# Second attention: four value products side by side for the first column half too, the odd key blocks' part collected on its own and added once per four head pairs

## What is computed

```python
def split_heads(y):
    return y.reshape(B, T, H, hd).transpose(0, 2, 1, 3)
q = split_heads(x @ Wq)          # H = 16 heads of hd = 16
k = split_heads(x @ Wk)
v = split_heads(x @ Wv)
scores = jnp.einsum('bhqd,bhkd->bhqk', q, k) / jnp.sqrt(jnp.float32(hd))
scores = jnp.where(causal, scores, jnp.float32(-jnp.inf))
attn = jax.nn.softmax(scores, axis=-1)
out = jnp.einsum('bhqk,bhkd->bhqd', attn, v)
```

## Time and profile before

| | |
|---|---|
| median of three runs | 853.15 us (852.07 to 854.26) |
| the profiled execution | 851.88 us, of which 850.1 us are its span |
| TensorE matmul | 759.7 us busy, 89% of the span |
| VectorE | 530.4 us, 62% |
| ScalarE | 430.0 us, 51% |
| GpSimd | 423.9 us, 50% |
| second attention, first exponential to last copy | about 487.6 to 619 us of the span |
| experts' block | from about 619.3 us |

### The profile page before, as it was taken

The page is one execution under the profiler, slowest core; times in us unless marked ns, Lnnn a source line. Parts: engine busy times, 40 slices in busy tenths (PEclk is TensorE's granted clock), DMA queues, the critical chain, the costliest instruction groups (busy, mean ns, idle before and its releaser), DMA issues. The chain is left out here.

```text
span 850.1 us, 12826 instructions
## 1 busy us (share of the span) xinstructions
PE 759.7 (89%) x3664; PEld 366.5 (43%) x3664; DVE 530.4 (62%) x1350; ACT 430.0 (51%) x922; POOL 423.9 (50%) x746
## 2 busy tenths in 40 slices
PE   2948999999999999984984798999889999999995
PEld 2332223222222222221752232333267888888883
DVE  3659777777777876603661876788147555555555
ACT  1431566665666665661133065767744554455552
POOL 1751556664334223422132032235368998689994
PEclk9975899999999999995888598999999999999997
DMA  6393740010011001012029374233232221122221
GB/s 186 128 295 87 156 103 18 25 55 20 15 47 40 14 22 58 17 46 71 1 94 272 119 181 122 72 110 117 79 84 80 66 69 60 39 68 67 62 63 58
DMA packets 60074, 69.82 MB, mean 82 GB/s; under 512 B 14904, under 2 KB 40857, under 8 KB 60010
## 3 DMA queue, kind: packets, MB, share of 16 engines
q1 hardware_dynamic: 59936, 69.08, 29.1%
q10 hardware_dynamic: 80, 0.07, 0.0%
HBM read 47.35 MB, written 15.47 MB: 74 GB/s over the span
## 5 line engine op out<-in xcount | busy, mean ns | idle before, releaser
L715 ACT ACTIVATE top<-ps 128x512 f32<-128x512 f32 (+3 forms) x384 | 171.0, 490 | 134.7 <-PE ps L662 134.5
L662 PE MATMUL ps<-mid 99*128 99x512 bf16 (+3 forms) x576 | 185.5, 338 | 8.4 <-ACT mid L715 5.4
L645 PE MATMUL ps<-mid 96*128 96x512 bf16 (+3 forms) x512 | 174.8, 364 | 13.8 <-PEq L233 9.6
L757 DVE CUSTOM_DVE_ANT_0 ps<-ps,keep 128x512 f32<-128x512 f32 (+3 forms) x320 | 162.0, 530 | 26.8 <-PE ps L645 26.4
L682 PE MATMUL ps<-top,mid 128*33 128x512 f32 (+3 forms) x768 | 162.1, 501 | 0.0
L1493 PE MATMUL ps<-xp,wp 128*128 128x512 f32 (+1 forms) x600 | 147.1, 394 | 4.7 <-ACT wp L1543 2.9
L662 PEld LDWEIGHTS ps<-mid 99*128 99x128 bf16 x576 | 54.2, 99 | 181.8 <-ACT top L715 103.7
L839 POOL TENSOR_SCALAR_AFFINE_SELECT top<-top 128x128 f32<-128x128 f32 x256 | 71.2, 291 | 110.9 <-ACT top L715 108.5
L1493 PEld LDWEIGHTS ps<-xp,wp 128*128 128x128 f32 (+1 forms) x600 | 112.5, 189 | 31.3 <-ACT xp L1545 3.4
L715 ACT ACTIVATE mid<-ps 128x512 f32<-128x512 f32 (+1 forms) x192 | 82.5, 493 | 67.2 <-PE ps L662 42.9
L761 DVE TENSOR_REDUCE top<-ps 128x1 f32<-128x512 f32 x128 | 88.4, 690 | 37.5 <-PE ps L645 36.8
(11 more groups left out here) (206 smaller groups left out, 818.5 us busy)
## 6 DMA issues: line engine op xcount, KB each, us to landing
mid<-part_scratch SPq DMA_DIRECT2D x9, 1152.0 KB, 8.8
part_scratch<-top SPq DMA_DIRECT2D x18, 384.0 KB, 5.0
top<-in_w SPq DMA_DIRECT2D x16, 396.0 KB, 3.9
cw_s<-combine_rows SPq DMA_DIRECT2D x48, 128.0 KB, 3.0
part_scratch<-top SPq DMA_DIRECT2D x18, 256.0 KB, 5.1
mid<-part_scratch SPq DMA_DIRECT2D x9, 384.0 KB, 4.0
top<-inverse_scratch SPq DMA_DIRECT2D x12, 256.0 KB
top<-in_w SPq DMA_DIRECT2D x8, 384.0 KB, 5.2
```

The lines of the kernel that those rows point to most:

```text
L645: nc.tensor.matmul(ps[:, s_bank(turn), 0:w], queries(pair, m)[0:PARTS, i * P:(i + 1) * P], keys(pair, m)[0:PARTS, c * 512:c * 512 + w], st ...
L662: nc.tensor.matmul(ps[:, ST_BANK + n % AHEAD, 0:w], keys(pair, m)[0:STACK, j * P:(j + 1) * P], queries(pair, m)[0:STACK, q0:q0 + w], start ...
L715: nc.scalar.activation(pr[:, n % RING, 0:w], ps[:, ST_BANK + n % AHEAD, 0:w], ACT.Exp, scale=0.25).then_inc(p_ready, 1)
L757: ins = nc.vector.tensor_tensor_reduce(bank, bank, msk[:, 512 - w:512], -1.0 if low else 1.0, 3e38 if low else -3e38, ALU.add, ALU.min if ...
```

## The change

In the second attention, half 0 is treated as half 1 was. Its value products of odd `j` go to quarters 2 and 3; its groups are four blocks wide and are issued in steps 5 and 9. The copy out of PSUM takes 128 rows instead of 64. `outputs` of half 0 issues eight DMAs instead of four; the odd part has no columns below 128, so that it is 384 columns wide and its denominators fill 12 rows of `cd` instead of 16 (the others are set to zero once, at the start). The odd parts are collected in a new tile `n0`, one for each `f`, and added at the end of four pairs: the denominators by VectorE in `inverted`, the numerators in `scale` (128x384). The counts of the semaphores follow, and `mrow` moves to another part of memory.

```diff
+                n0 = (sb("n0_even1", [P, 384], F32, here), oT[:, 3, 640:T])
...
-            PER = (64, 64) if first else (64, 128)
+            PER = (64, 64) if first else (128, 128)
...
-                for half in range(1 + c):
+                for half in range(2):
                     for m in range(2):
                         at, row = 32 * (m + 2 * half), 16 * (2 * h + m)
-                        to = second(f)[row:row + 16, :] if half else o1[row:row + 16, f, columns(c)]
-                        sp.dma_start(to, src[at:at + 16, :]).then_inc(outs[c], 16)
-                        sp.dma_start(cd[row:row + 16, c, half, :], src[at + 16:at + 17, :]).then_inc(outs[c], 16)
+                        skip = 128 if half and c == 0 else 0
+                        to = o1[row:row + 16, f, columns(c)]
+                        if half:
+                            to = (n0[f % 2] if c == 0 else second(f))[row:row + 16, :]
+                        sp.dma_start(to, src[at:at + 16, skip:512]).then_inc(outs[c], 16)
+                        sp.dma_start(cd[row + skip // 32:row + 16, c, half, :], src[at + 16:at + 17, skip:512]
+                                     ).then_inc(outs[c], 16)
...
-                if not first and c == 1:
-                    nc.vector.tensor_tensor(cd[:, 1, 0, :], cd[:, 1, 0, :], cd[:, 1, 1, :], ALU.add).then_inc(den_sum, 1)
-                    dve.wait_ge(den_sum, f + 1)
+                if not first:
+                    nc.vector.tensor_tensor(cd[:, c, 0, :], cd[:, c, 0, :], cd[:, c, 1, :], ALU.add).then_inc(den_sum, 1)
+                    dve.wait_ge(den_sum, 2 * f + c + 1)
...
-                if not first and c == 1:
-                    eng.tensor_tensor(to, to, second(f), ALU.add).then_inc(num_sum, 1)
-                    eng.wait_ge(num_sum, f + 1)
+                if not first:
+                    odd, part = (n0[f % 2], to[:, 128:512]) if c == 0 else (second(f), to)
+                    eng.tensor_tensor(part, part, odd, ALU.add).then_inc(num_sum, 1)
+                    eng.wait_ge(num_sum, 2 * f + c + 1)
...
-                GROUPS = [(b, b + 2) for b in range(0, 8 if not first else PAIR, 2)]
-                if not first:
-                    GROUPS += [(b, b + 4) for b in range(8, PAIR, 4)]
+                WIDE = 2 if first else 4
+                GROUPS = [(b, b + WIDE) for b in range(0, PAIR, WIDE)]
...
-                mrow = sb(f"mrow{layer}", [48, P], BF16, here)
+                mrow = sb(f"mrow{layer}", [48, P], BF16, here if first else keep)
...
-                                r0, v = 32 * (m + 2 * c * (j % 2)), vall[:, 2 * pair + m, j, :]
-                                start, stop = j <= c, j >= 4 * c + 3 - c
+                                r0, v = 32 * (m + 2 * (j % 2)), vall[:, 2 * pair + m, j, :]
+                                start, stop = j <= 1, j >= 4 * c + 2
...
-                            rows = P if first or c == 1 else 64
                             to = osb_odd if c == 1 else osb
-                            nc.scalar.copy(to[0:rows, :], ps[0:rows, ACC + c, :]).then_inc(o_evac, 1)
+                            nc.scalar.copy(to[:, :], ps[:, ACC + c, :]).then_inc(o_evac, 1)
...
+                        if not first:
+                            nc.gpsimd.memset(cd[:, 0, 1, :], 0.0).then_inc(cleared, 1)
...
                         ahead(0)
+                        if not first:
+                            sp.wait_ge(cleared, 3)
```

## The result

The changed kernel takes 864.09 us (median of 4 runs, 862.66 to 865.7) where the kernel before took 852.61 us beside it (4 runs, 850.27 to 854.26). The ratio is 1.0149 [1.0119, 1.0179]: slower by 11.5 us, where 3.4 were forecast (856.5 us) and 860.0 was the upper end of the range. Its profiled execution took 862.73 us, of which 861.0 are its span.

What follows compares the result with a forecast made beforehand. TensorE was taken to set a pair's pace, with the ring of eight holding its saving back and SyncE's queue the main cost. Terms -0.3 + 3.2 + 0.5 = +3.4 us on 853.15 gave 856.5 us, range 852.0 to 860.0.

Steps and rivals of the forecast that it cites:

- the same three terms: Pairs up to pair 6's maxima rows -0.3 us, end of the attention +3.2, experts +0.5: together +3.4.
- the clock: Rival: pair 4's stall or the pause ahead of the experts lowers TensorE's clock, costing 2.5 us, 859 us; chance 0.17.
- The ring: Second attention: exponential 8 waits for step 5's value group to free block 0's place, leaving 0.25 of 1.23 us per pair.
- the saving comes through whole: Rival: ScalarE isn't held at exponential 8, pairs gain 1.3 to 1.6 us each, 852.2 us; chance 0.13.
- Pairs 0 to 3: Second attention: pair 0 gains 0.7 us, pair 1 loses 0.3, pairs 2 and 3 gain 0.25 each; -0.9 in all.
- Pair 4: VectorE's wait for pair 3's half 0 outputs ends later, TensorE waits 0.55 us more, the gain is lost: +0.6 us.
- the prediction's three signs of being wrong: Pairs of 14.3 us, new issues under 0.5 us each, or TensorE's granted clock falling in the middle of the attention.
- The queue behind pair 4: SyncE's queue with both `inverses` takes 15.9 us against 15.3, so TensorE waits some 0.5 us for maxima rows (0 to 3).
- It fits: SyncE's 22 issues per pair take 13.6 us in all, against the pair's 15.3.
- Whatever its size: One output DMA costs 0.63 us of SyncE's queue, independent of its size.
- The end of the attention: SyncE's added output issues move the queue's end by 3.9 us; 0.7 is slack, so the experts begin 3.2 later.
- In the experts: VectorE's added sum of half 0's odd part stands before the last addition of half 1's parts: +0.5 us.

Runs made afterwards that it cites:

- experiment 1: Changed kernel with half 0's outputs as four DMAs again and its added sums left out, groups of four kept: 850.16 us, 1.0018 of the kernel before.
- experiment 2: As experiment 1, with a ring of nine exponentials instead of eight in the second attention: 845.95 us, 0.9951 of the kernel before.
- experiment 5: Changed kernel with both maps' denominators in one 32-row DMA, 18 issues per pair instead of 22: 854.93 us, 1.0046; its table sorts TensorE's waits in the experts.
- experiment 7: Changed kernel with a ring of nine instead of eight, nothing else that matters: 860.16 us, 1.0096 of the kernel before.
- the last kernel of experiment 8: Changed kernel with ring of nine, merged denominators and half 0's last sum made early, next pair's loads still in front of half 0's outputs: 847.77 us, 0.9992.
- experiment 4: Changed kernel without the last sum of half 0 (odd part left out for the last four pairs): 859.68 us, 1.0116 of the kernel before.

## Why the prediction was right in direction and wrong in size

The sum was -0.3 + 3.2 + 0.5 = 3.4; the same three terms measured 3.1 + 3.8 + 4.0 = 10.9. Four things in it failed: the added sum's price in the experts, the clock, which the sum had at nothing, the length of the queue behind pair 4, and the pairs' lead.

- **The ring: right.** Exponential 8 waits 1.33 us and a pair gains 0.24, forecast 0.25 (experiment 1); the ring of nine moves that limit (experiment 2). The rival "the saving comes through whole" is refuted by experiment 1, in which TensorE was busy 7.8 us less and the ratio was 1.0018.
- **Pairs 0 to 3: right by luck.** The difference is -1.1 us, forecast -0.9, but this execution of the changed kernel came to the attention 1.2 us ahead. From its first score product on, these four pairs gained nothing. Pair 0, for which I had -0.7, lost 0.4, as the clock came back later. The wait in pair 1 grew by 2.1 (2.74 to 4.85) and not by 0.3, and what it cost came back with the clock, which was at 1.00 again some 2 us sooner than before. When the clock comes back was in no term.
- **Pair 4: the clock failed, which had no term.** I had +0.6 for this pair, and its mark moved by 2.6 against pair 3's. The wait itself came out much as worked out: VectorE's ended at 562.39, and TensorE went on at 563.57, 0.23 us later than before (563.34), where I had 0.55 later. It was longer than forecast (1.90 us) because TensorE came to it ahead. The other 1.3 us to the mark, and some more behind it, are the clock (0.94 and 0.78, above). I had that as a rival at one place with 2.5 us, pair 4 or the pause ahead of the experts. It came at both, and at a third, behind the wait in the experts: 1.7, 0.6 and 1.5, 3.8 us in all, none of it in the sum. It was also the one of the prediction's three signs of being wrong that came.
- **The queue behind pair 4: mis-sized.** "It fits" held for the pairs without `inverses`. For the stretch behind pair 4 I had 15.9 us, and it lasted 17.25, of which the `inverses` took 3.2 (579.19 to 582.38), not 2.3; the same step had already taken 3.8 in the kernel before. It also began 1.55 late, since its rows waited for a pair that stood still itself. TensorE stood 1.64 us in pair 5, forecast 0.5, and pairs 5 and 6 lost 1.5 together instead of nothing. "Whatever its size" was wrong too, but it weighs little: a DMA of 12 rows holds the queue for 0.81 us and not 0.63, the one behind it for 0.57, some 0.24 us per pair together. The stated upper bound for this term, 3 us, held; the range had no room for it together with pair 4's and the clock.
- **The end of the attention: right as a mechanism,** 6.9 - 3.1 = 3.8 us from pair 6's mark to the experts' group, forecast 3.2; SyncE's twenty-four outputs have 0.24 of the difference. It came on top of the 3.1 that the pairs had lost by then, because ring, pairs and queue are in series. Experiment 5 takes the four issues away and with them both this term and most of the pairs' loss: 8.8 us.
- **In the experts: the largest miss.** I priced the added sum at +0.5 from a duration of 0.61, that is, from a place where GpSimd happened to be out of the way, and this part cost 4.0 us. TensorE's wait grew by 2.5. By the table of experiment 5 the sum alone is worth 1.55 of wait, and VectorE's start ahead of GpSimd's 1.48 without the sum; both together make the 2.50. The clock cost 1.5 in the group behind the wait and 0.6 in the first group (8.27 against 7.64). That makes 4.6, of which some tenths are absorbed. That the first group's 0.6 comes of the longer pause isn't shown: experiment 7 had the longest pause, 7.64 us, and its first group took 7.39. The prediction had no term for the rest; in the kernel before the same instruction takes 1.67 us next to 0.68, which I should have asked about. Experiment 1, with no added sum, has the slow form too and loses 2.4 us from the experts' first group to the end.
- **Coalescing.** The Trainium skill (DMA: Bandwidth & Descriptors, Rules for kernel authors) advises one large transfer in place of many small ones. Experiment 5 agrees on this kernel: four DMAs fewer per pair, with no fewer bytes, are worth 8.8 us. My reading is that the issue's time on SyncE's queue decided it; no run separates it from the landing.
- **4x for narrow outputs.** The Trainium skill (TensorEngine Tiling (Array Packing), Theoretical Speedup) holds for the groups alone, in which four products take 1.04 and 0.61 us as two did; TensorE's busy time fell by 6.4 us. None of it reached the end with a ring of eight (experiment 1).

By ratios the loss of 12.7 us is made up of 1.5 for the groups alone, 2.4 for the added sums and transfers (experiments 1 and 5) and 8.8 for the four issues. Only the last is clear of the intervals.

## What to carry to other kernels

Before the busiest engine is given less to do, ask who hands it its next input and from which buffer places: here the saving was worth nothing until the ring had one more place, and four DMA issues per pair cost more than both together gave. Count a DMA queue per stage and not on the mean, and price an added instruction on the critical path by the slowest row of its kind beside its neighbours, not by the fastest. A term in which TensorE will stand still longer needs the clock added to it. And count a difference between two traces from the first instruction that the change can reach: here 1.2 us of lead from ahead of it looked like a forecast that had come true.

## What was not expected of the hardware

- A DMA with 12 rows of denominators took 0.77 us of SyncE's queue to issue (611.53 - 610.72 to the next start: 0.81), one with 16 rows 0.59 and one with 32 rows 0.55, although that one moves most. The Trainium skill (DMA: Bandwidth & Descriptors, Why a DMA increments its semaphore by 16 and not by 1) has a candidate: the number of DMA engines is the largest up to 16 that divides the outer sizes of both sides, by which 12 rows get 12 at most, and the issuer itself writes the part of the increment that is missing. The rows agree with it in sign; no run here tests it.
- The same VectorE instruction of 128x512 took 0.68, 1.23 or 1.78 us, and GpSimd's of 128x256 0.72 or 1.19 us, depending on whether the other engine was at work. The Trainium skill (SBUF — State Buffer, SBUF: two separate sides) has a rule for it that I had not weighed: an addition of VectorE with both inputs in SBUF and a GpSimd instruction that reads SBUF lock each other out for a whole instruction. The timelines agree in part: where the two meet, the instructions grow, and whichever of the two at the combine rows begins first decides which one does (GpSimd's takes 0.72 or 1.19, experiment 5). That it is a lock and not a slow-down of both, they don't show.
- TensorE's clock doesn't follow from the length of a pause alone. After 2.40 us of waiting the next twelve products took 4.60 us in experiment 1, and after 2.41 us in experiment 2 too; after 2.39 us in the last kernel of experiment 8 they took 3.02, and after 2.41 us in experiment 4 too:

```profile
644.24 4.60 PE L1501 MATMUL ps<-xp,wp 128*128 128x512 f32 x12 [2.40 <-DVE g L1686]
```

```profile
640.85 3.02 PE L1505 MATMUL ps<-xp,wp 128*128 128x512 f32 x12 [2.39 <-DVE g L1690]
```
